# First-stage cross attention scores: one exact product, or three products of rounded and exact parts

## The reference

```
Q = x @ Wq ; K, V = context @ Wk, context @ Wv
energy = einsum('bqd,bkd->bqk', Q, K)              # 100 x 1444 for each batch
lengths = sum(energy[:, 0] != 0, axis=-1)           # scores of query 0 that are not exactly zero
energy = where(key index >= lengths, -inf, energy)
score = softmax(energy / sqrt(8)) ; z = einsum('bqk,bkd->bqd', score, V)
```

## Time and profile before

| | |
|---|---|
| median of 3 runs | 2285.15 us (2272.82 to 2285.22) |
| profiled execution, first to last instruction | 2267.4 us |
| PE, PEld busy | 87%, 55% of the span |
| DVE, ACT, POOL busy | 70%, 58%, 24% |
| mean granted clock of TensorE | 0.927 |
| loop of `stage_a` | about 134 to 399 us |
| score products L708 in it | 192 records, 92.9 us busy |

### The profile page before, as it was taken

How to read it: one execution, slowest core, us unless ns; L and a number is a source line. 1 busy time by engine, 2 the same in 40 slices (tenths; PEclk the granted TensorE clock), 3 DMA queues, 4 the chain that set the end, 5 groups by cost and what they waited for, 6 DMA issues and landing times. The chain is left out here.

```text
span 2267.4 us, 43146 instructions
## 1 busy us (share of the span) xinstructions
PE 1969.0 (87%) x16922; PEld 1258.0 (55%) x16922; DVE 1578.2 (70%) x3726; ACT 1324.7 (58%) x2169; POOL 551.4 (24%) x477
## 2 busy tenths in 40 slices
PE   3679999667999999999999999999997888888997
PEld 2546666444556556565565655556564555555554
DVE  4845666795787877878788788878771566664554
ACT  3645776683366666666666666666664555553444
POOL 1411322314122212222221222222222132311122
PEclk9879999777799999999999999999998788788999
DMA  5025554012132323233131322313222001103441
GB/s 153 1 92 183 184 173 142 4 37 91 65 109 74 126 68 118 78 105 119 68 126 63 120 85 101 121 66 122 79 89 67 16 8 16 31 1 59 67 71 40
DMA packets 120023, 189.26 MB, mean 83 GB/s; under 512 B 36770, under 2 KB 94090, under 8 KB 118414
## 3 DMA queue, kind: packets, MB, share of 16 engines
q1 hardware_dynamic: 119822, 186.50, 26.6%
HBM read 103.33 MB, written 11.76 MB: 51 GB/s over the span
## 5 line engine op out<-in xcount | busy, mean ns | idle before, releaser
L1610 DVE TENSOR_REDUCE b_part_max<-psum 128x1 f32<-128x482 f32 (+3 forms) x1248 | 737.6, 651 | 188.1 <-PE psum L1487 174.1
L1400 ACT ACTIVATE b_PT<-psum 128x800 f32<-128x800 f32 x768 | 616.6, 836 | 386.1 <-PE psum L1506 381.1
L1487 PE MATMUL psum<-b_KH,b_QBD 64*128 64x482 f32 (+1 forms) x1152 | 422.6, 445 | 45.7 <-DVE b_part_max L1610 43.3
L1506 PE MATMUL psum<-b_QS,b_KS 64*128 64x200 f32 x3072 | 438.3, 288 | 0.5 <-ACT b_PT L1400 0.3
L1506 PEld LDWEIGHTS psum<-b_QS,b_KS 64*128 64x128 f32 x3072 | 339.4, 186 | 16.2 <-issue 11.8
L1522 PE MATMUL psum<-b_PT,b_V 128*32 128x200 f32 x6144 | 341.4, 339 | 0.6 <-ACT b_PT L1400 0.6
L1487 PEld LDWEIGHTS psum<-b_KH,b_QBD 64*128 64x128 f32 x1152 | 197.3, 189 | 198.6 <-DVE b_part_max L1610 118.4
L1322 POOL TENSOR_TENSOR b_KL<-b_KF,b_KH 128x1444 fp32r<-128x1444 f32 x32 | 106.8, 3338 | 693.3 <-PE psum L1506 670.1
L1522 PEld LDWEIGHTS psum<-b_PT,b_V 128*32 128x32 f32 x6144 | 159.9, 109 | 149.1 <-ACT b_PT L1400 82.3
L1900 ACT ACTIVATE c_HE<-psum,C 128x400 f32<-128x400 f32 x128 | 75.7, 595 | 94.6 <-PE psum L2116 90.1
L1474 PE MATMUL psum<-W,b_CT 128*128 128x128 f32 (+1 forms) x768 | 117.7, 293 | 12.6 <-DVE b_part_max L1610 6.7
(11 more groups left out here) (280 smaller groups left out, 3095.2 us busy)
## 6 DMA issues: line engine op xcount, KB each, us to landing
b_KS<-b_KH SPq DMA_DIRECT2D x64, 722.0 KB
a_CT<-in_ctxt SPq DMA_DIRECT2D x32, 722.0 KB, 5.5
b_CT<-in_ctxt SPq DMA_DIRECT2D x32, 722.0 KB, 4.4
b_KS<-b_KL SPq DMA_DIRECT2D x32, 722.0 KB
a_CN<-in_ctxn SPq DMA_DIRECT2D x32, 704.0 KB
att_scratch<-b_AO SPq DMA_DIRECT2D x32, 200.0 KB, 1.9
c_G<-gates_scratch SPq DMA_DIRECT2D x4, 1600.0 KB
c_KBD<-gates_scratch SPq DMA_DIRECT2D x4, 1600.0 KB
```

Of the source, the lines that this page charges most:

```text
L1400: nc.scalar.activation(PT[:, kt % 2, 2 * a:2 * a + 2, :], psum[:, 2 * a:2 * a + 2, 0:TG], ACT.Exp).then_inc(sem["pt_ready"], 1)
L1487: m = mm(bank(b, D, size), QBD[rows, j % 2, tile * D:(tile + 1) * D], KH[rows, j % 2, at_:at_ + size], start=True, stop=True)
L1506: m = mm(bank(p, D, 2 * T, (s % 2) * 2 * T), KS[rows, j % 2, s, kt * D:(kt + 1) * D], QS[rows, j % 2, s * 2 * T:(s + 1) * 2 * T], start=Tr ...
L1610: v.tensor_reduce(part_max[0:rows, q, c:c + 1], bank(b, rows, CHUNKS[c][1]), AX.X, ALU.max)\
```

## The change

The scores of the first stage are no longer one exact float32 product. Keys and queries are each split into a high part, rounded to float32r by a copy on VectorE (`CTH`, `RTH`), and a low part, the difference to the exact value, computed on GpSimd and rounded as it is written (`CTL`, `RTL`). A score chunk is then three rounded products that add up in PSUM: low queries with high keys, high queries with low keys, high with high.

The keys are split for each batch (128x1446), the queries once for each unit (128x400). In the loop the VectorE copy for batch `m + 3` stands between the length of batch `m + 1` and `front(m)`, and so ahead of the maximum; the GpSimd subtraction stands ahead of its own `front(m)`. TensorE waits for the low parts instead of the key load; the load of keys `m + 1` waits for the subtraction of batch `m - 2` instead of its scores. The high and low parts have two places each; `AQ`, a buffer of the closing phase, now lies in the place of `CT`.

```diff
+        CTH = sb("CTH", [D, 2, SPAD], F32R)
+        CTL = sb("CTL", [D, 2, SPAD], F32R)
+        RTH = sb("RTH", [D, 2, TG], F32R)
+        RTL = sb("RTL", [D, 2, TG], F32R)
...
-        AQ = sb("AQ", [T, 2, INNER])
+        AQ = CT[0:T, 0, 0:2 * INNER].rearrange("p (m c) -> p m c", m=2)
...
                 if m + 1 < BATCH:
-                    sp.wait_ge(sem["s2_psum"], 3 * (m - 1))
+                    sp.wait_ge(sem["ctl_ready"], m - 1)
                     load_keys(m + 1)
...
+            def low_keys(m):
+                pool.wait_ge(sem["cth_ready"], m + 1)
+                pl.tensor_tensor(CTL[:, m % 2, :], CT[:, m % 3, :], CTH[:, m % 2, :].bitcast(F32), ALU.subtract).then_inc(sem["ctl_ready"], 1)
+
+            def low_queries(u):
+                pool.wait_ge(sem["rth_ready"], u + 1)
+                pl.tensor_tensor(RTL[:, u % 2, :], RT[:, u, :], RTH[:, u % 2, :].bitcast(F32), ALU.subtract).then_inc(sem["rtl_ready"], 1)
+
             ticks(((rstd(0), 0), (gain1, 3), (rstd(1), 2)), UNITS + 3)
+            low_queries(0)
+            for m in range(3):
+                low_keys(m)
             for m in range(BATCH):
+                if m % GROUP == 1 and m // GROUP + 1 < UNITS:
+                    low_queries(m // GROUP + 1)
+                if m + 3 < BATCH:
+                    low_keys(m + 3)
                 front(m)
...
-                    pe.wait_ge(ct_loaded[m % 3], (m // 3 + 1) * 16)
+                    pe.wait_ge(sem["rtl_ready"], u + 1)
+                    pe.wait_ge(sem["ctl_ready"], m + 1)
...
-                mm(bank(b, T, size), RT[:, u, t.ts_(j)], CT[:, m % 3, 512 * c:512 * c + size],
-                   start=True, stop=True).then_inc(sem["s2_psum"], 1)
+                keys, q = slice(512 * c, 512 * c + size), t.ts_(j)
+                mm(bank(b, T, size), RTL[:, u % 2, q], CTH[:, m % 2, keys], start=True, stop=False)
+                mm(bank(b, T, size), RTH[:, u % 2, q], CTL[:, m % 2, keys], start=False, stop=False)
+                mm(bank(b, T, size), RTH[:, u % 2, q], CTH[:, m % 2, keys], start=False, stop=True).then_inc(sem["s2_psum"], 1)
...
+            def high_keys(m):
+                dve.wait_ge(ct_loaded[m % 3], (m // 3 + 1) * 16)
+                if m >= 2:
+                    dve.wait_ge(sem["s2_psum"], 3 * (m - 1))
+                v.tensor_copy(CTH[:, m % 2, :], CT[:, m % 3, :]).then_inc(sem["cth_ready"], 1)
+
+            def high_queries(u):
+                dve.wait_ge(sem["rT2_ready"], UNITS)
+                if u >= 2:
+                    dve.wait_ge(sem["s2_psum"], 3 * GROUP * (u - 1))
+                v.tensor_copy(RTH[:, u % 2, :], RT[:, u, :]).then_inc(sem["rth_ready"], 1)
+
+            high_queries(0)
+            high_keys(0)
+            high_keys(1)
             for part in range(3):
                 last = count(0, part)
             link(last)
             length(0)
+            high_keys(2)
             top(0)
...
                     link(count(m + 1, 2))
                     length(m + 1)
+                if m % GROUP == 1 and m // GROUP + 1 < UNITS:
+                    high_queries(m // GROUP + 1)
+                if m + 3 < BATCH:
+                    high_keys(m + 3)
                 front(m)
                 if m + 1 < BATCH:
                     top(m + 1)
```

More of the change, by code:

```diff
@@ L106 @@
 A_SIGNALS = """
-a_chain a_cleared a_out_ready aqT_psum aqT_ready aq_ready down_psum e1T_psum e1T_ready e1_ready e2_ready eg_ready
+a_chain a_cleared a_out_ready aqT_psum aqT_ready aq_ready cth_ready ctl_ready down_psum e1T_psum e1T_ready e1_ready e2_ready eg_ready
 f1_psum f1_ready f2_psum factors_ready gu_psum gu_used hout_ready inner_ready len1_psum len1_ready len2_ready
-max2_ready pT_psum pT_ready quant_ready r2_psum rT2_ready rT_ready r_psum row_ready s1_psum s2_psum s2m_psum scaled1
+max2_ready pT_psum pT_ready quant_ready r2_psum rT2_ready rT_ready r_psum row_ready rth_ready rtl_ready s1_psum s2_psum s2m_psum scaled1
 scaled2 scaled3 sm1_ready v1_psum v1_ready y1_ready y2_ready y3_ready z1_psum z2T_psum z2T_ready z2_psum
```

## The result

The changed kernel took 2311.88 us (median of 4 runs, 2307.03 to 2319.2) beside 2285.18 (4 runs, 2272.82 to 2285.81) of the kernel before on the same chip: ratio 1.015, 95% interval 1.0118 to 1.0182. The medians are 26.7 us apart, while a ratio of 1.015 is 34 us: the four executions of the kernel before were three of 2285 to 2286 and one of 2273. A repeat (e5) gave 1.0152 and medians 31.8 apart. Forecast were 2320, 34.9 more than before, and a range of 2286 to 2352.

The account below looks back on a forecast made before the run. It took a per-batch ring of dependent steps as the bound, nearly level with TensorE's program. 17.6 + 8.7 + 7.2 - 3.2 + 4.6 = +34.9 us on 2285 gave 2320, range 2286 to 2352.

Parts of the forecast that it names:

- the 100x4 steps: Ends of VectorE's moments routines in the loop: wait out GpSimd's 3.34 us key subtraction, stretched from 0.17 to 1.5-3 us.
- kinds 1 and 2: Loop batches with VectorE work before the maximum, a residual in kind 1: +2.9 us each (six), +1.75 each (five).
- Kind 0: Five loop batches with outcome step, fc1 product and value projection: outcome first, then GpSimd; +1.45 us each, +7.2 in all.
- The case in which GpSimd wins: Kind 0 batches: GpSimd's subtraction starts before the outcome step, which begins at 6.15 us; at most +1.9 us more each.
- The copy: VectorE's rounding copy of 128x1446 keys between length and maximum: two columns at a time, 0.91 us.
- My rival's figures: Loop, only the copy's own length counts: kind 1 +1.15 us, kind 2 +0.35; +9 in all, 2294; chance 0.15.
- The other batches: 16 batches, kind 3 and the first and last: copy and subtraction fit idle time, 0.2 us won each, -3.2.
- the clock rival: TensorE idles 2 to 3 us in 16 batches and its clock falls to half: +24 us, 2344; chance 0.13.
- The products: Score chunks on TensorE: three rounded products for one exact; TensorE wins 0.45 to 0.62 us a batch, 0.6 taken.
- the ring: Each batch's chain from last score chunk through count, length, cut, maximum, exponent: 7.90 us, sees 0.2 of the products' gain.
- The rival in which TensorE is the bound: Loop: TensorE gets its full 0.6 us in each of 32 batches, -15 us, 2270; chance 0.10.
- The opening: Before the loop: first product waits for copies and subtractions, 5.8 us, less 1.2 won by its products: +4.6.

Follow-up runs that it names:

- e5: The changed kernel run once more, unaltered, beside the kernel before: 2310.95 us, ratio 1.0152 to the kernel before.
- e1: Changed kernel with each 100x4 scalar step of the moments in loop and closing phase written as four 100x1 steps: 2291.09 us, 1.0055 to the kernel before.
- e2: Changed kernel with GpSimd's key subtraction cut to 8 of 1446 columns from batch 2 on: 2282.99 us, 1.0008 to the kernel before.
- e8: e7 with kind 3's high copy left behind the length and keys 0 and 1 split mid-opening: 2290.96 us, 1.0062 to the kernel before.
- e3: Changed kernel with key copy and subtraction left out from batch 2 on, rounded products kept: 2279.56 us, 0.9994 to the kernel before.
- e9: e8 with kind 0's key subtraction waiting for outcome's moments from batch 12, query copy and subtraction moved: 2272.18 us, 0.9968 to the kernel before.
- e10: e9 with a fourth rounded product, low queries with low keys, in each score chunk: 2293.56 us, 1.0076 to the kernel before.
- e6: Changed kernel with the places of high and of low keys 1448 columns apart instead of 1446: 2314.62 us, 1.0153 to the kernel before.
- e11: e9 with the key subtraction's two inputs always 8 bytes apart in address modulo 16: 2273.3 us, 0.998 to the kernel before.
- e7: Changed kernel with the high key copy ahead of the third count, three high and two exact key places: 2296.05 us, 1.0069 to the kernel before.

## Why the prediction was right, and where its steps were off

- **What decides**, the 100x4 steps that wait until GpSimd is done with the maximum queued behind them: shown, by the row itself, by e1 (another form of step, no wait) and by e2 (no long subtraction, no wait). The Trainium skill (SBUF — State Buffer, Who interferes with whom) calls this an exclusive lock, held for the whole instruction. The trace agrees: the subtraction ends at 237.67, the 100x4 step beside it at 237.70.
- **Sizes of kinds 1 and 2** came out a quarter to a third lower (12.3 for 17.6, 6.4 for 8.7). In kind 2 (9.5 us a batch for 9.9) the mis-sized term is the subtraction: I took 3.34 us, and it is 2.75 in three of the five batches, 3.25 in two. In kind 1 (10.35 for 11.05) it is 3.25 in four of six and only part of the miss. In batch 9 the maximum came 6.86 us behind the last chunk for 7.45: 0.3 of that because the subtraction began earlier, since the query subtraction ran beside the key copy (1.63 us from 232.83) and not behind it, 0.1 by its length, and 0.2 because the maximum followed its end by 0.01. The rest, 0.2 a batch in kind 1 and 0.1 in kind 2, is my count from chunk to chunk, where the table counts from exponent to exponent.
- **Kind 0**: 4.2 for 7.2. That outcome goes first was right (263.69 before 263.85). But I let the subtraction wait for its end, from 3.45 us; it started 0.16 behind outcome, at 2.75, and lost only 0.45 (3.19 or 3.70 for 2.75 or 3.25), so the batches took 9.7 us for 10.6. The case in which GpSimd wins, up to 1.9 a batch more, did not happen here; e8 showed it at 1.9 to 3.2 a batch over batch 8's 8.40, or 0.25 to 1.55 over the same batches of the changed kernel.
- **The copy**: 0.915 us forecast as 0.91. Where it stands it costs 0.8 us in kind 1 and 0.5 in kind 2 even without any wait (e2 less e3, undisturbed batches). My rival's figures were against the kernel before, 1.15 and 0.35; there e2 is 1.0 and 0.1 longer.
- **The other batches**: +1.0 for -3.2, right only where undisturbed, 0.27 and 0.36 us quicker for 0.2. Batch 0 took 9.35 us for 8.19: the granted clock was 0.61 from 143 to 158 us, where before it was 1.00 from 146 us on. All kernels with three products show this (9.35 to 9.79), and my sum had nothing for it. Two more, 6 and 11, behind long ones, took 9.30 and 10.28 us. That is the clock rival, coming true in a few places in place of everywhere: from 250 to 256 us TensorE ran at about 1.2 GHz, after a stretch in which it was busy 70%. Columns as in the earlier trace rows:

```profile
245.00:250.00 5.00, 3.49 (x27) 2.86 (x25) 4.89 (x15) 2.83 (x7) 4.67 (x4) 1.00 0.08 22
250.00:256.00 6.00, 5.17 (x20) 4.25 (x21) 1.89 (x6) 3.08 (x6) 4.58 (x3) 0.51 0.69 230
```

  Over the same batches in e9 they lost 1.5 and 2.7 us, 4.1 of the 24 that I gave the rival if it held everywhere; batches 14, 18, 22 and 26 have some of it inside the sum of kind 2.
- **The products**: three of 512 columns start 0.23 us apart at the full clock, as forecast, but the first is 0.29 ahead of the second, and a chunk takes 0.76. In the batch of the earlier trace rows TensorE wins 0.37 us (2.33 to 1.96 in e9), for the 0.6 that I took. All score products together are busy 89.0 us for 92.9 (82.0 in e9, where the clock stays up), and TensorE was busy 89% of the loop where I had written 75. That the ring sees 0.2 us a batch came out about right (0.27 to 0.36) by a wrong reading. I took count, length and cut row as the only way to the cut; TensorE's list was as late, and there every chunk counts (e10). The rival in which TensorE is the bound was thus half right, in a segment I had not looked at; that the two errors, 0.6 for 0.37 and one chunk for three, nearly cancel is luck.
- **The opening**: +5.0 for +4.6, behind the last copy of RT (5.7 in e5 and e6). From the stage's start to the first exponent it is 5.9 to 8.6 us longer in all kernels with the split than in the one trace of before (120.6). In e1 and e6 the part up to the last copy of RT is as before (110.7 for 110.45), in the changed kernel's trace 3.0 longer; whether that is due to the change or to chance stays open.
- **The total**: 28.9 us in loop and opening; timed 26.7 by the first medians, 31.8 by e5's, 34 by the ratio; 34.9 forecast. Part of this closeness is luck: the three kinds came out 10.6 below their terms, and the other batches, mostly by the clock in 0, 6 and 11, gave 4.2 back. And I added the 35 to 2285.15, where later medians of the kernel before are 2277 to 2280.

## What to carry to other kernels

- Before putting a long GpSimd operation beside VectorE work, list which VectorE steps run in its time and what is queued behind each: here steps of 0.17 us cost some 20 us in 16 batches, because the longest chain of the kernel stood behind them.
- Who comes first decides. The GpSimd instruction queued directly behind the one that VectorE waited for won in all five kind 0 batches of e8; one wait on GpSimd (e9, which also moves the query parts) gave 19 us.
- If a step of a ring is released by two things at once, as the cut here, test how far either may move before counting on a gain.

## What the runs showed of the hardware that was not expected

- The form of a tiny VectorE step decides whether it waits: a tensor_scalar of 100x4, SBUF to SBUF, took up to 1.79 us for 0.17; four of 100x1 took 0.34 together in the same place. It is not the shape alone: in batch 9 of e8 a reciprocal of 100x4 took 0.15 us at 227.24, in the midst of a key subtraction from 226.65 to 229.92, and statistics, aggregations and a scalar_tensor_tensor that reads PSUM and SBUF (1.13 for four) kept their length beside a subtraction too.
- GpSimd's subtraction of 128x1446 float32 takes 2.74 us or 3.25 us by where its inputs lie. Places 1446 columns apart are 5784 bytes apart, 8 modulo 16. If all three buffers begin alike modulo 16, which I infer and did not read from anywhere, the slow ones in the changed kernel, e6 and e9 are those whose inputs lie alike; with the inputs 8 bytes apart in all (e11) 32 of 32 are quick.
- The same wait strikes GpSimd: the query subtraction takes 1.63 us beside the key copy and 1.03 alone (e7, e8), and two key subtractions in the opening with VectorE copies beside them took 7.11 us together, for 6.5.
